# An attention and expert layer in fp32: the softmax reciprocals through 32-square transposes, and the weighted sums in two visits a step

## The reference

```
attn = einsum('bhdq,bhdk->bhqk', qh, kh)
attn = softmax(s * attn, axis=-1)
out  = einsum('bhqk,bhdk->bhdq', attn, vh)
x = x + out
x = x + moe(layernorm(x), Wg, w1, w2)     # top 2 of 8 experts, relu, 512 -> 2048 -> 512
```

## Time and profile before

| | us |
| --- | --- |
| median of 3 runs | 2165.97 |
| lowest and highest | 2164.49, 2166.17 |
| the profiled execution's own time | 2168.21 |
| its span, first to last instruction | 2166.5 |
| TensorE busy | 2102.9 (97%) |
| VectorE busy | 1000.6 (46%) |
| ScalarE busy | 700.2 (32%) |
| GpSimd busy | 474.2 (22%) |
| mean granted TensorE clock | 0.994 of full |

### The profile page before, as it was taken

How to read it: one execution, slowest core, us unless ns; L and a number is a source line. 1 busy time by engine, 2 the same in 40 slices (tenths; PEclk the granted TensorE clock), 3 DMA queues, 4 the chain that set the end, 5 groups by cost and what they waited for, 6 DMA issues and landing times. The chain is left out here.

```text
span 2166.5 us, 27115 instructions
## 1 busy us (share of the span) xinstructions
PE 2102.9 (97%) x10179; PEld 1524.5 (70%) x10179; DVE 1000.6 (46%) x1908; ACT 700.2 (32%) x1216; POOL 474.2 (22%) x596
## 2 busy tenths in 40 slices
PE   3999999999999999999999999999999999999997
PEld 1455555555548888878888887888888788888875
DVE  5678888788764344234324323423432342243211
ACT  1566666566642222112212212211311231122110
POOL 3334444443432012010301301021030012101101
PEclk9999999999999999999999999999999999999999
DMA  9787777787645337114414612523431252241101
GB/s 147 153 174 173 172 164 183 161 187 170 140 135 161 98 79 158 21 22 110 107 21 97 137 21 60 129 48 58 110 86 27 56 135 54 44 127 30 19 4 20
DMA packets 183895, 216.61 MB, mean 100 GB/s; under 512 B 39731, under 2 KB 111419, under 8 KB 183740
## 3 DMA queue, kind: packets, MB, share of 16 engines
q1 hardware_dynamic: 154128, 173.21, 34.9%
q0 software_dynamic: 22240, 37.92, 8.9%
q10 hardware_dynamic: 7372, 3.42, 0.7%
HBM read 113.93 MB, written 68.29 MB: 84 GB/s over the span
## 5 line engine op out<-in xcount | busy, mean ns | idle before, releaser
L1607 DVE SCALAR_TENSOR_TENSOR hlo<-ps_h,hhi 128x512 fp32r<-128x512 f32 x256 | 177.0, 691 | 928.2 <-ACT hhi L1484 872.1
L1484 ACT ACTIVATE hhi<-ps_h 128x512 fp32r<-128x512 f32 x256 | 152.9, 597 | 1123.5 <-PE ps_h L1748 1104.8
L1746 PE MATMUL ps_h<-xhi,w1hi 128*128 128x512 f32 x1024 | 404.7, 395 | 2.6 <-PEq L1333 1.4
L1765 PE MATMUL ps_y<-w2hi,hhi 128*128 128x512 f32 x1024 | 404.4, 395 | 0.7 <-DVE hlo L1607 0.7
L1766 PE MATMUL ps_y<-w2lo,hhi 128*128 128x512 f32 x1024 | 402.9, 393 | 1.2 <-issue 1.2
L1748 PE MATMUL ps_h<-xhi,w1lo 128*128 128x512 f32 x1024 | 403.5, 394 | 0.0
L1767 PE MATMUL ps_y<-w2hi,hlo 128*128 128x512 f32 x1024 | 403.5, 394 | 0.0
L1747 PE MATMUL ps_h<-xlo,w1hi 128*128 128x512 f32 x1024 | 402.8, 393 | 0.0
L686 DVE TENSOR_REDUCE nmax<-ps_s 128x1 f32<-128x512 f32 x512 | 333.3, 678 | 121.8 <-PE ps_s L1107 120.3
L463 ACT ACTIVATE probs<-ps_t 128x512 f32<-128x512 f32 x504 | 265.8, 607 | 144.6 <-PE ps_t L1053 132.0
L1746 PEld LDWEIGHTS ps_h<-xhi,w1hi 128*128 128x128 f32 x1024 | 192.3, 188 | 48.6 <-issue 2.7
(11 more groups left out here) (204 smaller groups left out, 1991.9 us busy)
## 6 DMA issues: line engine op xcount, KB each, us to landing
raw<-in_L_ffn_w SPq DMA_DIRECT2D x128, 512.0 KB
qst<-qhi SPq DMA_DIRECT2D x64, 256.0 KB, 7.8
xin<-dispatched SPq DMA_DIRECT2D x60, 256.0 KB, 5.9
kst<-khi SPq DMA_DIRECT2D x52, 256.0 KB, 7.1
xt<-in_x SPq DMA_DIRECT2D x32, 256.0 KB, 3.1
ct<-in_ctx SPq DMA_DIRECT2D x32, 256.0 KB, 4.7
qst<-qlo SPq DMA_DIRECT2D x32, 256.0 KB, 8.8
xres<-in_x SPq DMA_DIRECT2D x32, 256.0 KB, 5.1
```

The lines of the kernel that those rows point to most:

```text
L1484: nc.scalar.activation(hhi[k % 2][:], ps_h[k % 3][:], ACT.Relu).then_inc(hhi_ready, 1)
L1607: nc.vector.scalar_tensor_tensor(hlo[k % 2][:], ps_h[k % 3][:], 0.0, hhi[k % 2][:].bitcast(F32), ALU.max, ALU.subtract).then_inc(h_ready, 1)
L1746: nc.tensor.matmul(to, w1hi[:, c, fs], xhi[n % 2][:, c, :], start=(c == 0), stop=False)
L1765: nc.tensor.matmul(ps_y[b][:], hhi[k % 2][:, bs], w2hi[:, f, :], start=(f == 0), stop=False)
```

## The change

The round trip through DMA and TensorE goes. VectorE transposes ps_l in squares of 32 x 32 (`sums_turned`), which brings the four heads' sums of 32 positions into one column of each square; it takes the reciprocal of these columns alone, 128 x 16 (`reciprocals`), and transposes them back, each read 32 times over, into 128 x 512 (`spread`). The product with `o_sb` (`scaled`) now stands at (2, 3) of the same step, one step earlier than before, and the residual waits for it. The buffers, the matmul `shares`, its bank turn, three DMAs a step and the copy L545 go, and so do some constants' setup on GpSimd and ScalarE.

TensorE's visits are now two a step with two chunks each: chunks 2 and 3 of group s - 3 behind c = 0, and chunks 0 and 1 of group s - 2 behind c = 2. `probs` has four buffers. `x_scaled` keeps its place at (0, 3), ahead of the new transposes; the statistics of the residual's rows move to (2, 3) and (3, 1). In the tail the same holds: `weighted` behind c = 0 and c = 2, with the last group's chunk 2 alone behind its c = 3.

```diff
+NPROBS = 4
-            if c == 1 and live(s - 4):
-                s_turn["r", s - 4] = len(s_turn) + 1
...
             def residual(g):
-                pool.wait_ge(s_free, s_turn["r", g])
+                pool.wait_ge(o_scaled, g + 1)
...
-                if i == 0 and n >= 3:
-                    act.wait_ge(pv_done, n - 2)
-                nc.scalar.activation(probs[n % 3][:, i, :], t_at(k)[:], ACT.Exp).then_inc(t_free, 1)
+                if i == 0 and n >= NPROBS:
+                    act.wait_ge(pv_done, n - NPROBS + 1)
+                nc.scalar.activation(probs[n % NPROBS][:, i, :], t_at(k)[:], ACT.Exp).then_inc(t_free, 1)
...
                     if c == 0 and live(s - 3):
-                        g = s - 3
-                        act.wait_ge(l_done, g + 1)
-                        if g >= 2:
-                            act.wait_ge(l_ld[g % 2], 16 * turns(g - 2, 2))
-                        nc.scalar.activation(l_sb[g % 2][:], ps_l[:], ACT.Copy).then_inc(l_saved, 1)
-                        sums_out(g)
+                        sums_out(s - 3)
...
+            def sums_turned(g):
+                dve.wait_ge(l_done, g + 1)
+                if g >= 1:
+                    dve.wait_ge(r_found, g)
+                nc.vector.transpose(l_turned[:], ps_l[:].rearrange("p (b j) -> p b j", j=Q)).then_inc(l_saved, 1)
+
+            def reciprocals(g):
+                dve.wait_ge(l_saved, g + 1)
+                if g >= 1:
+                    dve.wait_ge(r_spread, g)
+                nc.vector.reciprocal(r_few[:], l_turned[:, :, 0]).then_inc(r_found, 1)
+
+            def spread(g):
+                dve.wait_ge(r_found, g + 1)
+                if g >= 1:
+                    dve.wait_ge(o_scaled, g)
+                nc.vector.transpose(r_rows[:], r_few[:].unsqueeze(2).to_broadcast([P, D // Q, Q])).then_inc(r_spread, 1)
...
-                        if (c, i) == (3, 1) and live(s - 4):
+                        if (c, i) == (2, 3) and live(s - 4):
                             g = s - 4
                             dve.wait_ge(x1_ready, g + 1)
                             nc.vector.bn_stats(st2[g % 2][:, 0:6], x1[g % 2][:]).then_inc(stat2, 1)
-                        if (c, i) == (3, 2) and live(s - 4):
+                        if (c, i) == (3, 1) and live(s - 4):
...
+                        if (c, i) == (0, 3) and live(s - 5):
+                            x_scaled(s - 5)
+                        if (c, i) == (0, 3) and live(s - 3):
+                            sums_turned(s - 3)
+                            reciprocals(s - 3)
+                            spread(s - 3)
+                        if (c, i) == (2, 3) and live(s - 3):
+                            scaled(s - 3)
...
-            def weighted(g, c):
-
-                n = 4 * g + c
-                pe.wait_ge(t_free, t_turn["t", g, c, HPG - 1])
-                if c == 0:
+            def weighted(g, chunks):
+
+                pe.wait_ge(t_free, t_turn["t", g, chunks[-1], HPG - 1])
+                if chunks[0] == 0:
                     pe.wait_ge(t_free, t_turn["vt", g])
                     if g >= 1:
                         pe.wait_ge(o_saved, g)
+                    products(g, chunks)
+                    if g >= 1:
+                        pe.wait_ge(l_saved, g)
+                    row_sums(g, chunks).then_inc(pv_done, len(chunks))
                 else:
+                    summed = row_sums(g, chunks)
+                    if chunks[-1] == NC4 - 1:
+                        summed.then_inc(l_done, 1)
+                    products(g, chunks).then_inc(pv_done, len(chunks))
...
-                    if c == 1 and live(s - 4):
-                        shares(s - 4)
                     if c == 0 and live(s - 3):
-                        weighted(s - 3, NC4 - 1)
-                    if c > 0 and live(s - 2):
-                        weighted(s - 2, c - 1)
+                        weighted(s - 3, (2, 3))
+                    if c == 2 and live(s - 2):
+                        weighted(s - 2, (0, 1))
```

More of the change, by code:

```diff
@@ L97, in bank_turns @@
     t_turn["x2t", G - 1] = len(t_turn) + 1
-    for key in (("r", G - 4), ("logits", G - 5), ("places", B - 2), ("logits", G - 4), ("logits", G - 3),
+    for key in (("logits", G - 5), ("places", B - 2), ("logits", G - 4), ("logits", G - 3),
                 ("places", B - 1), ("logits", G - 2), ("places", B), ("logits", G - 1), ("places", B + 1), "total"):
@@ L141, in attention_and_dispatch @@
         kst = [xin[:, :, 0:D] if i == XIN_AT else sb(f"kst{i}", [P, HPG, D], F32R) for i in range(KR)]
-        probs = [sb(f"probs{i}", [P, HPG, D]) for i in range(3)]
+        probs = [sb(f"probs{i}", [P, HPG, D]) for i in range(NPROBS)]
         vt = [sb(f"vt{i}", [P, NC4, P]) for i in range(4)]
@@ L153, in attention_and_dispatch @@
         o_sb = [sb(f"o_sb{i}", [P, D]) for i in range(2)]
[L154 to L160, removed]
+        l_turned = sb("l_turned", [P, D // Q, Q])
+        r_few = sb("r_few", [P, D // Q])
+        r_rows = sb("r_rows", [P, D // Q, Q])
         x1 = [sb(f"x1_{i}", [P, D]) for i in range(2)]
@@ L476, in sums_out @@
                 nc.scalar.activation(o_sb[g % 2][:], ps_o[:], ACT.Copy).then_inc(o_saved, 1)
-            def sums_spread(g):
-                act.wait_ge(l_saved, g + 1)
-                if g >= 2:
[L481 to L490, removed]
-                                  ).rearrange("h (c q) -> h c q", c=LW),
-                                  r_hl[g % 2][:, part, :].bitcast(F32)).then_inc(r_ld[g % 2], 16)
             def row_turned(g):
@@ L554, in _ @@
                         nc.scalar.activation(qhi[g % 2][:], qf[:], ACT.Copy).then_inc(qhi_ready, 1)
-                    if c == NC4 - 1 and live(s - 3):
-                        shares_in(s - 3)
-                if s == 0:
-                    act.wait_ge(dims_made, 5)
-                    for part in range(2):
-                        act.dma_start(to_dims[HPG * part:HPG * part + HPG, :].bitcast(F32), dims[:]).then_inc(dims_st, 16)
                 if 1 <= s <= FILLS // 2:
@@ L707, in _ @@
                             nc.vector.bn_aggr(st2[g % 2][:, 6:8], st2[g % 2][:, 0:6]).then_inc(var2, 1)
-                        if (c, i) == (0, 3) and live(s - 5):
-                            x_scaled(s - 5)
                         if (c, i) == (1, 1) and live(s - 1):
@@ L913, in _ @@
             maxima_turned(G - 1)
-            reciprocal(G - 3)
-            weighed(G - 4)
             rows_added(G - 4)
+            sums_turned(G - 3)
+            reciprocals(G - 3)
+            spread(G - 3)
             logits_out(G - 5)
@@ L920, in _ @@
             counted_on(B - 2)
-            weighed(G - 3)
+            scaled(G - 3)
             rows_added(G - 3)
@@ L926, in _ @@
             x_scaled(G - 3)
-            reciprocal(G - 2)
-            weighed(G - 2)
+            sums_turned(G - 2)
+            reciprocals(G - 2)
+            spread(G - 2)
+            scaled(G - 2)
             rows_added(G - 2)
@@ L938, in _ @@
             places_out(B - 1, (B - 2) % 2, 0, 2)
-            reciprocal(G - 1)
-            weighed(G - 1)
+            sums_turned(G - 1)
+            reciprocals(G - 1)
+            spread(G - 1)
+            scaled(G - 1)
             rows_added(G - 1)
@@ L1069, in values @@
                 done.then_inc(t_done, 1)
-            def shares(g):
-                pe.wait_ge(r_ld[g % 2], 32 * turns(g, 2))
-                if g == 0:
-                    pe.wait_ge(dims_st, 32)
-                bank = s_bank(s_turn["r", g])
-                nc.tensor.matmul(bank[:], to_dims[:], r_rows[g % 2][:], start=True, stop=True).then_inc(s_done, 1)
             def logits(g):
@@ L1144, in _ @@
                     turned_logits(g, c, 1)
-                    if g == G - 2 and c == 0:
-                        shares(G - 4)
-                    weighted(g if c else g - 1, (c - 1) % NC4)
+                    if c == 0:
+                        weighted(g - 1, (2, 3))
+                    if c == 2:
+                        weighted(g, (0, 1))
+                    if c == 3 and g == G - 1:
+                        weighted(g, (2,))
                     if c == 0:
```

103 lines of the change are left out of this document (25 added, 78 removed).

## The result

In runs on the same chip the kernel before took 2170.43 us (median of 7, 2164.49 to 2171.91) and the changed one 2157.66 us (median of 7, 2153.56 to 2159.74). The ratio is 0.995, 95% interval 0.9935 to 0.9965: **faster by 0.35 to 0.65%, 7.6 to 14 us**. Forecast were 2150 us, a ratio of 0.993 to the 2165.97 of then. The sign and the range held, and most of the mechanism; the gain is 0.5% where 0.7% was forecast. The profiled execution is the fastest of the seven, 2153.56 us with a span of 2151.8. That is 14.7 less than the 2166.5 of before, where the medians differ by 12.8.

A forecast was written before the change was run, and what follows sets the result against it. TensorE, busy 99.8 of 100 us, was taken to bound the steps. The terms -15.7 + 7.8 + 2.1 - 9.6 - 1.85 - 0.2 = -17.4 gave 2150.8 us, or 2148.6 from the median; forecast 2150, range 2142 to 2167.

The forecast's parts named there:

- TensorE's order: In each attention step, merged visits and removed work shorten TensorE's sequence from 12.27 to 11.71 us: -15.7 over 28 steps.
- The new waits: At c = 2, TensorE waits 0.28 us for ScalarE every step (+7.8) and 0.15 more for VectorE in odd steps (+2.1).
- The transposes: VectorE's two new transposes take 0.70 us each; with a reciprocal of 0.25 the chain of 1.6 us is just hidden.
- The first rival: VectorE's new transposes cost 1.09 us each, so S of (1, 3) waits: +10 us, 2160; chance 0.2.
- The irregular time: In 25 attention steps, 9.6 us of irregular time come from the DMA round trip and go with it: -9.6.
- the second rival: Irregular step time isn't the round trip's alone, other transfers are late too; only half of 9.6 us goes: 2158, chance 0.12.
- Slower by clock dips at c = 2: Two close waits of 0.3 us in odd steps each bring a lowered TensorE clock: +24 us, 2174; chance 0.14.
- Start and tail: One visit less at the start saves 1.85 us; the tail's extra chunk is offset by savings and waits: -1.85 in all.
- End: At the attention stage's end a 3.36 us reciprocal becomes a 1.65 us chain, but GpSimd's queue lets only 0.2 arrive: -0.2.
- The step that failed: The expert stage is untouched, so whatever the attention stage gains carries to the end one for one.

The follow-up runs named there:

- the longer chain: The changed kernel with `spread`, VectorE's second transpose, done twice in each step: 2174.03 us, a ratio of 1.0016 to the kernel before.

## Why the prediction was right, and where it was wrong

- **TensorE's order**, -0.56 a step: right. Gaps were 0.04 shorter than forecast each, which is most of why steps came out at 17.47 and 18.19 where the terms give 17.60 and 18.33.
- **The new waits**: 0.24 for ScalarE (0.28) and 0.20 in odd steps for VectorE, each at its place. A third of 0.08, at the S of (0, 3), was not seen.
- **The transposes**: 0.71 (0.70), reciprocal 0.25 (0.25); hidden, with 0.20 to spare at 323.70. The first rival falls. The rule of the Trainium skill that the prediction weighed (SBUF — State Buffer, the note on cachelines under "Door 1: The DMA port swizzle") agrees, 0.71 in order and 1.10 at a stride of 16 bytes, though L1587 differs in writing PSUM too, and no run parts the two.
- **The irregular time**, -9.6: right in its cause, which the second rival doubted, but a number of one execution; two others had 22.7 and 9.0. The 25 steps gained 17.6 where the earlier trace rows and the step terms give 14.8. Its support was misread, since TensorE waited 2.8 us and not 11.2 for `r_rows`; of the 25 steps' time it was idle for 5.2, and the rest of the 9.6 stands behind the waits.
- **Slower by clock dips at c = 2**: didn't come. In the changed kernel waits of 0.24 and 0.20 were followed by a clock of 1.00. A wait of 0.60 in its second profile was followed by one of 0.63. And four of the experiments ran into it, with a clock of 0.91 to 0.98 in the steps and ratios up to 1.022. Splitting both visits or the second leads there, an earlier copy of the keys does, and so do merged visits beside the old trip. Whether the changed kernel escapes this rival for a reason or by luck is open, since no run shows what decides when the clock falls.
- **Start and tail**, -1.85: no gain at the start can be seen (126.41 and 127.04 with the old order against 126.74 and 127.54), and the tail is wrong in sign. It lost 1.5 us. Its visit at 594.69 waited 1.28 for ScalarE, and behind it the clock was 0.83. The prediction had made "its waits for ScalarE about the rest", a term taken from the tail of before, where visits of one chunk waited 0.47; a merged one waits for the later chunk's exponentials.
- **End**, -0.2: GpSimd's queue held as said, its root beginning at 630.20 behind its scatters though VectorE was done at 628.8. That the lead still rose from 18.7 to 20.4 is mostly the clock: the ten fillers there took 1.36 us after and 2.48 before.
- **The step that failed** is the sentence that the expert stage is untouched and the gain carries to the end one for one. 20.2 us arrived at its door and 14.7 at the end. Its code is the same but its time isn't: two waits called issue (2.2 us) for one (1.2), a first tile at a lowered clock (18.3 for 16.7), and ten tiles at 89.49 where before had three (3.0). The second profiles say the same, 1309.3 against 1302.2. That more fillers take the waits away is shown; what sets the tiles is open.

## What to carry to other kernels

When an engine is 90% busy beside the bounding one, don't price work on it by the sum: ask which stretch of the bounding engine covers it. Here a removal and a merging that each lose 2% alone gain 0.5% together, so such edits have to be tried as pairs. Before moving an operation, look at what it hands on: a copy 1 us earlier started GpSimd beside VectorE's small operations and cost 2.7% (1.018 against 0.991, both with the one-hot moved). A stage that "isn't touched" is still a term with a spread of its own, 1299.4 to 1310.8 us over the fourteen profiles here. And a sum of waits over a matmul and its weight load isn't time that TensorE lost: ask for the matmul's row alone.

## What was not expected of the hardware

- The same wait of 0.42 to 0.46 us on TensorE was followed by a clock near half in five of twelve steps of one kernel, and in none of the eleven steps of the longer chain that have it.
- In the kernel with merged visits and the old trip the clock fell to 0.53 in a step with no wait over 0.2 us.
- Three operations on VectorE of 0.15 to 0.18 us (L703, L709, L721) take 0.72 to 1.03 beside a GpSimd operation of 1.28 us on SBUF, while L707 keeps its time.
- Two spacings of the same matmul, 0.2319 and 0.2331 us, at the same granted clock, each held over many tiles.
- Waits called issue, 0.8 to 2.0 us, went with eight fillers more, far from where they stood.
- VectorE was idle for about 1 us ahead of one small copy, and TensorE's wait behind it ends with VectorE's queue: in two steps of the changed kernel's second profile, and in six and ten steps of two kernels near it, always at the same place of the code.
